# Four attention layers over eight graphs: row maxima written as bf16, and the last head's sums and values on four 32-column tiles

## The reference, cut to what matters

```python
# layer 2 (and layer 3 with another mask), per graph
q, k, v = heads(x @ Wq.T + bq), heads(x @ Wk.T + bk), heads(x @ Wv.T + bv)   # 8 heads of 32
logits = q @ k.T / sqrt(32) + log(clip(adj, 1e-8))
out = softmax(logits) @ v
x = layer_norm(x + merge(out) @ Wo.T + bo, gamma, beta)
# layer 3 weighs softmax(logits + 2 adj - 1) by 0.25 + 0.75 adj, normalizes again, and ends in a feed-forward part
```

## Time and profile before

| | |
|---|---|
| median of three runs | 4613.52 us (4610.3 to 4614.56) |
| the profiled execution | 4611.31 us, of which 4609.4 us from the first to the last instruction |
| PE busy | 4116.9 us (89%) |
| DVE busy | 3374.8 us (73%) |
| ACT busy | 2078.8 us (45%) |
| POOL busy | 1945.7 us (42%) |
| granted TensorE clock, mean | 0.938 of full speed |

### The profile page before, as it was taken

One profiled execution on the slowest core, in us unless ns is written; L12 is line 12 of the kernel. 1 busy time (PEld: TensorE's weight loads), 2 busy tenths in 40 slices (PEclk: granted clock), 3 DMA queues, 4 the chain that ended last, 5 costly groups with the idle time before them and its releaser, 6 DMA issues.

```text
span 4609.4 us, 67131 instructions
## 1 busy us (share of the span) xinstructions
PE 4116.9 (89%) x20528; PEld 2171.0 (47%) x20528; DVE 3374.8 (73%) x4576; ACT 2078.8 (45%) x3654; POOL 1945.7 (42%) x1016
## 2 busy tenths in 40 slices
PE   7998899888998889988899898998989989899898
PEld 5534365343753337433374333743347433474334
DVE  3798737987379874898648986489855898558893
ACT  3264532645336543364433644236443365434553
POOL 1174601746026560265503655036540365404562
PEclk9998999989999899998999989999999999999999
DMA  3201102011020110201101011120111101111010
GB/s 106 71 19 33 51 20 65 19 33 51 24 60 19 35 49 29 58 17 35 49 32 54 17 35 49 33 56 15 38 49 35 51 15 38 51 37 49 15 37 16
DMA packets 109068, 180.41 MB, mean 39 GB/s; under 512 B 28256, under 2 KB 51040, under 8 KB 108704
## 3 DMA queue, kind: packets, MB, share of 16 engines
q1 hardware_dynamic: 108704, 175.89, 13.3%
HBM read 83.12 MB, written 8.39 MB: 20 GB/s over the span
## 4 chain that ended last, share of the span: by engine, by line
PE 41%; issue 21%; DVE 18%; POOL 15%; ACT 2%; DVEq 0%; DMA 0%; SPq 0%; POOLq 0%; ACTq 0%
POOL region_p L1352 12%; PE ps L529 11%; DVE row_max L1097 8%; PE ps L521 8%; PE ps L577 8%; DVE region_p L1089 5%; PE ps L726 4%; PE ps L618 3%; PE ps L566 2%; PE ps L637 2%; DVE sums_t L1071 1%; PE ps L602 1%; POOL rstd L1362 1%; POOL y_t L1414 1%; DVE region_p L1145 1%
## 5 line engine op out<-in xcount | busy, mean ns | idle before, releaser
L1352 POOL TENSOR_TENSOR region_p<-region_p,mask 128x1024 f32<-128x1024 f32 x592 | 1505.1, 2558 | 458.2 <-ACT region_p L848 457.8
L848 ACT ACTIVATE region_p<-ps 128x512 f32<-128x512 f32 x2048 | 1111.8, 595 | 765.1 <-PE ps L602 763.2
L1097 DVE TENSOR_REDUCE row_max<-ps 128x1 f32<-128x1024 f32 x1024 | 1201.8, 1211 | 67.7 <-PE ps L618 66.6
L637 PE MATMUL ps<-region_p,shelf 128*64 128x512 f32 x4096 | 1077.8, 607 | 75.3 <-DVE region_p L1089 63.5
L1089 DVE TENSOR_TENSOR region_p<-region_p,mask 128x1024 f32<-128x1024 f32 x432 | 744.4, 1727 | 34.5 <-ACT region_p L848 31.9
L618 PE MATMUL ps<-region_k,region_q 96*64 96x512 bf16 x4096 | 673.1, 416 | 65.4 <-DVE row_max L1097 60.6
L602 PE MATMUL ps<-region_q,region_k 97*64 97x512 bf16 x4096 | 672.5, 401 | 4.4 <-ACT region_p L848 2.6
L618 PEld LDWEIGHTS ps<-region_k,region_q 96*64 96x64 bf16 x4096 | 205.3, 114 | 630.5 <-DVE row_max L1097 376.8
L1362 POOL TENSOR_TENSOR rstd<-var_eps,minus_half 128x2 f32<-128x2 f32 (+1 forms) x160 | 117.6, 735 | 883.0 <-DVE var_eps L1052 883.0
L602 PEld LDWEIGHTS ps<-region_q,region_k 97*64 97x64 bf16 x4096 | 238.8, 113 | 407.1 <-ACT region_p L848 200.3
L637 PEld LDWEIGHTS ps<-region_p,shelf 128*64 128x64 f32 x4096 | 283.2, 139 | 285.1 <-DVE region_p L1089 101.5
(11 more groups left out here) (150 smaller groups left out, 4620.9 us busy)
## 6 DMA issues: line engine op xcount, KB each, us to landing
mask<-in_adj SPq DMA_DIRECT2D x64, 512.0 KB, 7.3
mask<-in_adj_t SPq DMA_DIRECT2D x64, 512.0 KB, 3.5
y_t<-o_raw SPq DMA_DIRECT2D x256, 64.0 KB, 2.0
sums_t<-o_raw SPq DMA_DIRECT2D x256, 64.0 KB, 2.0
region_q<-region_p SPq DMA_DIRECT2D x192, 64.0 KB, 2.0
region_k<-region_p SPq DMA_DIRECT2D x192, 64.0 KB, 2.0
region_q<-sums_t SPq DMA_DIRECT2D x192, 64.0 KB, 2.0
region_k<-sums_t SPq DMA_DIRECT2D x192, 64.0 KB, 2.0
```

Of the source, the lines that this page charges most:

```text
L637: last = nc.tensor.matmul(ps[64 * c:64 * c + 64, 6 + i, :], values_and_one, probs[:, t % RING, c * HALF:(c + 1) * HALF], start=(t == 0), s ...
L848: nc.scalar.activation(probs[:, t % RING, c * HALF:(c + 1) * HALF], ps[:, 4 + c, :], ACT.Exp, scale=DK ** -0.5).then_inc(exp_done, 1)
L1097: nc.vector.tensor_reduce(row_max[i][:, t:t + 1], flat[:, (t % 2) * N:(t % 2 + 1) * N], AX.X, ALU.max)\
L1352: nc.gpsimd.tensor_tensor(p, p, mask[:, t, :], ALU.mult).then_inc(masked_pool, 1)
```

## The change

It has two parts. **Maxima:** `maximum` writes bf16 itself; `cast_maxima`, `row_max` and their semaphore are gone, and PE's transposition waits for the last maximum. **The last head of a layer:** its products stand on four 32-column tiles (values of both halves, then sums of both halves). DVE inverts the 64 partitions of sums straight from PSUM into `o_raw` and multiplies the values in PSUM by them into `o_t` (`last_head`); ACT's copy, SP's four DMAs and 32 partitions of the other inversions and of POOL's products go. The inversions of the sums of heads 4 to 6 move: in the second layer between the masks of head 7, in the first layer to the end of head 7, ahead of the two mask steps that stand behind it. In head 7 POOL has tiles 1, 3, 4 and 6, one more than before. The next graph's adjacency loads wait for the last product and no longer for ACT's copy.

```diff
-POOL_TILES[H - 1] = (1, 3, 5)
+POOL_TILES[H - 1] = (1, 3, 4, 6)
...
+                        if h == H - 1:
+                            sp.sem_inc(o_moved[1], 64)
+                            continue
...
+                    sp.wait_ge(pv_done, att(b, 1, (0, H - 1), T, T))
                     for t in range(T):
                         load_adjacency(b, t)
...
+                        if i == 0:
+                            pe.wait_ge(o_last, b * 2 + layer + 1)
+                        else:
+                            pe.wait_ge(o_out, att(b, layer, (0, H - 1), 1, 1))
...
-                pe.wait_ge(max_cast, att(b, layer, h, 1, 1))
+                pe.wait_ge(max_done, att(b, layer, h, T, T))
...
+                if number(h) == H - 1:
+                    for kind in range(2):
+                        for c in range(2):
+                            r = 2 * DK * kind + DK * c
+                            last = nc.tensor.matmul(ps[r:r + DK, 6 + i, :], values_and_one[:, kind * DK:(kind + 1) * DK],
+                                                    probs[:, t % RING, c * HALF:(c + 1) * HALF],
+                                                    start=(t == 0), stop=(t == T - 1))
+                    last.then_inc(pv_done, 1)
+                    return
...
-                    take_sums(b, layer, (0, H - 1), 1)
...
+            def last_head(b, layer):
+
+                inverse = o_raw[1][0:2 * DK, :]
+                dve.wait_ge(pv_done, att(b, layer, (0, H - 1), T, T))
+                then(nc.vector.reciprocal(inverse, ps[2 * DK:4 * DK, 7, :]))
+                for c in range(2):
+                    part = nc.vector.tensor_tensor(o_t[P - DK:P, 1, c * HALF:(c + 1) * HALF], ps[DK * c:DK * (c + 1), 7, :],
+                                                   inverse[DK * c:DK * (c + 1), :], ALU.mult)
...
-                nc.vector.tensor_reduce(row_max[i][:, t:t + 1], flat[:, (t % 2) * N:(t % 2 + 1) * N], AX.X, ALU.max)\
+                nc.vector.tensor_reduce(row_max_bf[i][:, t:t + 1], flat[:, (t % 2) * N:(t % 2 + 1) * N], AX.X, ALU.max)\
...
-                nc.vector.tensor_copy(row_max_bf[i][:, :], row_max[i][:, :]).then_inc(max_cast, 1)
...
-                    head(b, layer, (0, H - 1), 1, False, make_early_mask if layer == 0 else None)
+                    def invert_half(t):
+                        if t == 5:
+                            heads_moved(b, layer, 1)
+                        if t in (5, 7):
+                            half = (t - 5) // 2
+                            invert_sums(1, slice(half * HALF, (half + 1) * HALF)).then_inc(inverted, 1)
+
+                    head(b, layer, (0, H - 1), 1, False, invert_half if layer else make_early_mask)
+                    if layer == 0:
+                        for t in (5, 7):
+                            invert_half(t)
+                    last_head(b, layer)
```

More of the change, by code:

```diff
@@ L1281, in whole @@
                             make_mask3(b, t)
-                    heads_moved(b, layer, 1)
-                    for half in range(2):
-                        invert_sums(1, slice(half * HALF, (half + 1) * HALF)).then_inc(inverted, 1)
                     dve.wait_ge(residual, b * 3 + layer + 1)
```

25 lines of the change are left out of this document (12 added, 13 removed).

## The result

The changed kernel takes **4586.38 us** (4586.07 to 4587.35, five runs), the kernel before 4611.11 us (4609.71 to 4614.56, five runs beside them): a ratio of 0.9946 [0.9932, 0.9959], 24.7 us less. The profiled execution took 4587.35 us, its span is 4585.5 us.

A forecast was written before the change was run, and what follows sets the result against it. DVE and POOL taking turns at one access was taken to bound the heads; casts 0, second layer 8 x (-1.6) and first layer 8 x 1.6 summed to 0, so 4613 us, range 4592 to 4634.

The forecast's parts named there:

- The taking of turns: Heads 0 to 5: DVE's operations from SBUF and POOL's masks alternate at one access, 14.9 us per head.
- The first layer's end: First layer, up to the first addition: DVE's masks wait beside POOL's, 1.6 us lost in each graph.
- Both slower rivals: Last head's four tiles run as two pairs, 4630 (16%); second layer's mask 5 goes after POOL's tile 6, 4632 (8%).
- the second one: Rival: the first layer's end loses nothing and PE restarts quicker in the second layer, 4597 us; 16%.
- Part 1, the casts at 0: Heads: removing 96 casts of 1.13 us each, 108 us of DVE time, gains 0.
- The cover: Heads: POOL's next mask holds the access until 238.68, so DVE's mask ends no earlier without the cast.
- The first rival: Heads: removed casts give time back, each head 0.24 us shorter through PE's wait for a maximum, 23 us, 4590; 12%.
- Part 2, second layer, 1.6 us: Second layer's end: PE goes on at 546.7 against 548.44, less 0.14, so 1.6 us saved in each of eight graphs.
- The 0.3 for two changes of column width: Second layer's end: two changes between 64 and 32 columns ahead of tile 4's exponential, 0.16 us each, cost 0.3.
- The sum: Whole kernel: 0 + 8 x (-1.6) + 8 x 1.6 = 0, so no change, about 4613 us; given 48%.
- Everything behind the addition hangs on it: First layer: all work behind the first addition follows it, so its 1.6 us loss counts in each graph.
- my own signs: Prediction wrong if a head's period changes by over 0.1 us or either layer end differs by over 1.2 us from forecast.

The follow-up runs named there:

- the experiment: The changed kernel with the last head's products on two 64-column tiles and one DVE inversion of all 128 partitions: 4581.47 us.
- the maxima alone: The kernel before with only the first part of the change, maxima written as bf16 and no casts: 4587.99 us.
- three added products: The changed kernel with three more 32x512 products on DVE ahead of the first layer's first addition: 4614.12 us; with filling 4536.06 and 4537.06 us.
- filling: The changed kernel with added PE work that changes no result, in three versions: 4531.11, 4516.80 and 4504.37 us.
- POOL's old tiles: The changed kernel with POOL's tiles of head 7 as before the change (1, 3 and 5): 4583.81 us.
- two column tiles and the old tiles: The changed kernel, filled more, with the last head on two 64-column tiles and POOL's head 7 tiles 1, 3 and 5: 4490.70 us.

## Why the prediction was wrong

**What held.** The taking of turns: the first mask grew to 2.35 us, and DVE is no less busy. The first layer's end: 1.6 us longer forecast, 1.5 measured, with the mask steps waiting beside POOL as described; but the 5.39 us of PE's keys that I took from the earlier trace rows as their price were in part at half clock, and against keys of 3.70 the loss is 3.2. Four column tiles run side by side, mask 5 comes ahead of POOL's tile 6, and the inversion from PSUM costs what one from SBUF does. Both slower rivals fell, and so did the second one, since the first layer did lose its 1.5 us.

**Part 1, the casts at 0: mis-sized.** They are worth 0.44 to 0.50 us a layer, about 0.07 a head and some 7.5 us over 16 layers. The cover, POOL's second mask, is there. But DVE's mask was asked for only about when POOL ended; now it stands in line, and POOL's pause is 0.07 us shorter. I put the mask's end at 239.76 after 239.78, a difference of 0.02. The first rival (23 us, through PE's wait for a maximum) had the sign for another reason. What the Trainium skill says ("VectorE: DVE Perf Modes", Rules for kernel authors) of fewer operations is borne out in sign, though by the rows what is saved is 0.07 us of a pause, not the cast's 1.13.

**Part 2, second layer, 1.6 us: mis-sized**, 2.1 to 2.3 at the clock that both kernels have there. In the first graph, less 1.35 us, I had mask 5 done at 533.25, the inversions at 536.55 and 540.95, `last_head`'s at 544.35; they ended at 533.10, 536.35, 540.68 and 544.08, each 0.15 to 0.3 early. The 0.3 for two changes of column width came on top; that the change of width costs something is likely (0.39 us in the experiment, of which the clock and the other inversion have an unknown part), but the rest of the path was shorter than I had it. "TensorEngine Tiling (Array Packing)" in the Trainium skill, Key Properties, says that changing the tiling mode drains TensorE: that it costs time the experiment agrees, by at most 0.2 and 0.4 us an end; a drain as such no run shows. At full clock the end is worth only 0.93: by these two graphs more than half of the 2.2 us is PE's time at half clock.

**The sum: the step that failed most.** "Everything behind the addition hangs on it" took a gain or loss ahead of a stage as a gain or loss of the graph, and nothing more. By the table's means the touched stages gave -0.70 + 1.53 - 0.44 - 2.20 = -1.81 us a graph, 14 us in eight, and the untouched ones -0.86 - 0.72 = -1.58 more. Of these, 0.49 is the order of turns in the norms, of which 0.13 is left at full clock. 0.36 in the first projections and 0.5 to 0.7 in the long stretch are the clock's: at full clock the projections do not differ, and the stretch takes 221.65 us before and 221.42 or 221.64 with the change. Without these 12.6 us in eight graphs the time would have been about 4599, inside the range.

PE's first work behind a pause ran at full clock where it had run at half; the time at half clock hardly differs (69.6 and 68.3 us a graph), but other work stands in it. I had the clock in no term, and no order of turns behind an end, though the clock's mean, 0.938 of full, stood in the table of the profile. That the clock can do this is shown by the maxima alone (1.6 us at an end that they do not touch, of which 1.3 are work at half clock), that both together can, by three added products (17 us of work, 28 us of time without filling, 5 and 20 with). By my own signs, a head's period within 0.1 us (from the third on; the first two of a layer moved by 0.07 to 0.20) and either end within 1.2 us, the mechanisms passed while the sum did not: the signs left out the stages behind.

Put together from full-clock rows alone, the change would not be a gain: -0.50 and -0.44 in the heads, +3.2 at the first layer's end, -0.93 at the second's and -0.13 in the norms make +1.2 us a graph. This is an estimate from stages of different runs and graphs; no run has a whole graph at full clock. By it the 24.7 us come on balance from where the clock falls and from the order of turns.

What stays open: whether it is chance that the time of a graph comes out at the same few values (566.6 us with the change and with POOL's old tiles; 570.0 before and with three more products), what decides the order of turns in the norms, and which pauses of PE the clock answers. The runs show that it happens, not the rule.

## What to carry to other kernels

Where PE pauses in many places and its granted clock falls in some, a change of a few us moves the falls, and a stage that nobody touched can gain or lose as much as the edit: read the granted clock of each stage before and after, and judge an edit in a stage at full clock on both sides. An instruction that waits for a shared access need not be free when its cover stays: ask whether the next one could have stood in line earlier. And look at filling the pauses themselves: work for PE that changes nothing took 82 us here (4586.4 to 4504.4), three times the change, and with two column tiles and the old tiles 4490.7 us is the fastest kernel here.

## What was not expected of the hardware

- Filling took the heads of a layer from 101.2 (second layer; 102.2 in the first) to 98.7 us and their clock from 0.93 to 1.00. In the fourth graph before, the first head had 0.59 and the second 0.80 of full clock; the clock fell where PE waits for DVE's maxima, 0.74 and 0.51 us at a time.
- Time at half clock costs nearly half of itself where PE sets the pace: 54.99 us at 0.94 (2 x 0.06 x 54.99 = 6.6 us at half clock) against 52.08 at 1.00. The Trainium skill ("TensorE: Matmul & The Clock Gate", HAM oscillation — how this bites in real kernels) counts half of the throttled time as lost; these rows come near it (2.91 of 6.6). Where other engines set the pace it is less: the unfilled kernel before has 10.8 us at half clock in that stretch (53.78 us at 0.90) and loses 1.7.
- Eight records on four 32-column tiles last 1.06 us, where four records on two 64-column tiles last 1.08, yet the kernel that does without the mix of both widths has ends that are 0.2 and 0.4 us shorter.
- A graph's time can stay the same to 0.1 us while one of its stages becomes 0.9 us shorter (old tiles: 566.6 us a graph, as with the change).
